# A two-layer graph kernel: ScalarE and TensorE programs written out instead of looped, with constant wait values

## What is computed

```python
def _L1_gnn_ref(x, spatial_encoding, edge_encoding, Wq, Wk, Wv, Wo):
    q = (x @ Wq.T).reshape(d, n, h)          # d = 128 heads, n = 3327, h = 8
    k = (x @ Wk.T).reshape(d, n, h)
    v = (x @ Wv.T).reshape(d, n, h)
    a = jnp.einsum('dnh,dmh->dnm', q, k) * scale
    a = a + spatial_encoding + edge_encoding
    a = jax.nn.softmax(a, axis=2)
    out = jnp.einsum('dnm,dmh->dnh', a, v)
    return out.reshape(n, h * d) @ Wo.T

h = jnp.maximum(_layernorm(x), 0.0);  x = x + _L0_gnn_ref(h, adj, L0_gnn_weight)
h = jnp.maximum(_layernorm(x), 0.0);  x = x + _L1_gnn_ref(h, adj, adj, Wq, Wk, Wv, Wo)
```

## Time and profile before

| | us |
|---|---|
| median of three executions | 14501.24 |
| lowest and highest | 14498.21, 14502.49 |
| the profiled execution, its own time | 14506.74 |
| its span, first to last instruction | 14504.7 |

### The profile page before, as it was taken

How to read it: one execution, slowest core, us unless ns; L and a number is a source line. 1 busy time by engine, 2 the same in 40 slices (tenths; PEclk the granted TensorE clock), 3 DMA queues, 4 the chain that set the end, 5 groups by cost and what they waited for, 6 DMA issues and landing times. The chain is left out here.

```text
span 14504.7 us, 430687 instructions
## 1 busy us (share of the span) xinstructions
PE 13822.4 (95%) x143755; PEld 4902.7 (34%) x143755; DVE 13807.1 (95%) x27589; ACT 13447.5 (93%) x30466; POOL 326.7 (2%) x945
## 2 busy tenths in 40 slices
PE   3889999999999999999999999999999999999999
PEld 2533333333333333333333333333333333333334
DVE  5589999999999999999999999999999999999993
ACT  1269999999999999999999999999999999999997
POOL 1100000000000000000000000000000000000000
PEclk7989999999999999999999999999999999999999
DMA  8965655656565565656556565655656565565653
GB/s 277 258 161 136 143 134 136 142 133 141 135 144 133 138 141 134 141 135 143 135 137 141 134 139 135 143 134 137 141 134 140 135 143 134 136 142 135 143 133 94
DMA packets 2075309, 2084.40 MB, mean 144 GB/s; under 512 B 818906, under 2 KB 1827809, under 8 KB 2066753
## 3 DMA queue, kind: packets, MB, share of 16 engines
q1 hardware_dynamic: 2069118, 2043.41, 58.8%
q10 hardware_dynamic: 4032, 13.31, 0.2%
HBM read 1922.23 MB, written 133.76 MB: 142 GB/s over the span
## 5 line engine op out<-in xcount | busy, mean ns | idle before, releaser
L235 DVE CUSTOM_DVE_ANT_0 X<-X,adj_row 128x832 f32<-128x832 f32 x13312 | 13314.5, 1048 | 111.8 <-PE X L257 74.7
L1000 ACT ACTIVATE prob<-S 128x416 f32<-128x416 f32 x26624 | 11895.8, 518 | 304.0 <-PE S L1068 121.7
L1068 PE MATMUL S<-q_blk,k_res 52*128 52x416 f16 x26624 | 6858.3, 344 | 41.5 <-ACT S L989 9.9
L1089 PE MATMUL O<-prob,v_pad 128*32 128x208 f32 (+1 forms) x87376 | 6727.3, 389 | 2.6
L257 PE MATMUL X<-mk,mq 40*128 40x416 f16 x26624 | 6270.4, 344 | 306.7 <-DVE m_part L235 279.8
L1068 PEld LDWEIGHTS S<-q_blk,k_res 52*128 52x128 f16 x26624 | 2214.9, 93 | 4250.3 <-ACT S L989 1454.4
L1089 PEld LDWEIGHTS O<-prob,v_pad 128*32 128x32 f32 x87376 | 1830.5, 108 | 2537.5 <-issue 2053.0
L257 PEld LDWEIGHTS X<-mk,mq 40*128 40x128 f16 x26624 | 1585.8, 93 | 2370.6 <-DVE m_part L235 1919.1
L235 DVE DVE_READ_ACCUMULATOR2_ANT m_part<- 128x1 f32 x13312 | 1884.5, 142 | 0.0
L989 ACT ACTIVATE S<-adj_key 128x416 f32<-128x416 f32 x3328 | 1757.2, 528 | 35.7
L207 POOL TENSOR_SCALAR m_neg<-m_full 128x16 f32<-128x16 f32 x208 | 52.5, 252 | 13065.5 <-DVE m_full L218 13065.4
(11 more groups left out here) (86 smaller groups left out, 1045.7 us busy)
## 6 DMA issues: line engine op xcount, KB each, us to landing
adj_key<-adj_by_key SPq DMA_DIRECT2D x3328, 208.0 KB, 3.4
adj_row<-in_adj SPq DMA_DIRECT2D x1200, 416.0 KB, 3.9
mk<-k_planes SPq DMA_DIRECT2D x1664, 104.0 KB
adj_row<-adj_tail SPq DMA_DIRECT2D x400, 416.0 KB, 3.9
mk<-k_planes SPq DMA_DIRECT2D x1664, 52.0 KB
row<-in_adj SPq DMA_DIRECT2D x47, 1663.5 KB, 8.0
adj_by_key<-aT SPq DMA_DIRECT2D x26, 1664.0 KB, 11.8
q_planes<-q_parts SPq DMA_DIRECT2D x26, 1024.0 KB, 15.0
```

The lines of the kernel that those rows point to most:

```text
L235: nc.vector.tensor_tensor_reduce(out=x_, in0=x_, in1=adj_row[gi % 4][:].rearrange("p (a b) -> p a b", a=2), scale=1.0, scalar=LOW, op0=ALU ...
L1000: nc.scalar.activation(prob[c % QR][:, d % 4, :], S[b][:, 0:WB], ACT.Exp, scale=2.0).then_inc(s_e[b], 1)
L1068: nc.tensor.matmul(S[b][:, 0:WB], k_res[base:base + KR, d // 2, s * P:(s + 1) * P], q_blk[n % 2][base:base + KR, d // 2, :], start=False, ...
L1089: done = nc.tensor.matmul(O[32 * d:32 * d + 32, cols], v_pad[:, s, 4 * q + d, :], prob[born(j, q) % QR][:, d, cols], start=first, stop=Tru ...
```

## The change

ScalarE and TensorE no longer call `spans` but `all_spans`, in which `k` is always a Python integer. Their programs become five times the loop's body and the tail; all their wait values become constants. SyncE keeps its loop, VectorE and GpSimd are as they were. The order of the matmuls, activations and DMAs, the semaphores and the values waited for stay the same.

```diff
+                def all_spans(first, last, body):
+
+                    for k in range(NG // 3):
+                        body(k, first, first + SPAN, 4 * SPAN)
+                    body(NG // 3, first, last, END)
+
...
-                        spans(act, FIRST, FIRST + END, body)
+                        all_spans(FIRST, FIRST + END, body)
...
-                        spans(pe, FIRST, FIRST + END + 8, body)
+                        all_spans(FIRST, FIRST + END + 8, body)
```

## The result

| | before | changed |
|---|---|---|
| median | 14499.5 us (15 runs) | 14533.9 us (15 runs) |
| lowest to highest | 14493.4 to 14513.7 | 14528.9 to 14541.8 |
| the profiled execution | 14506.7 | 14530.5 |
| its span | 14504.7 | 14528.1 |

The changed kernel takes 1.0024 times the time of the one before, with a 95% interval of 1.0016 to 1.0031: it is slower by 34 us. The forecast was 14526 us, in a range of 14505 to 14560; I had given 29% to slower by over 0.2%, and 60% to within it.

What follows compares the result with a forecast made beforehand. No single engine bounds it: TensorE, VectorE and ScalarE hand work round a ring. Added waits 58.0 us less returns 33.2 us gives +24.8 us on 14501.2: 14526 us, range 14505 to 14560.

Steps and rivals of the forecast that it cites:

- Part 1: TensorE's four loop returns: their stalls go, taking four segments from 460.0 to 426.8 us together, a gain of 33.2 us.
- boundary segments: The four stretches of 104 units between ScalarE output copies that hold a loop return; forecast from 460.0 to 426.8 us together.
- Part 2: TensorE's 32 ns and ScalarE's 35 ns register operations go; up to 3% if on the ring, but measured rate spoke against gain.
- Part 3: Constant waits give ScalarE two more separate semaphore waits a cycle before exponentials: 0.50 us a segment, adding 58 us.
- the added waits: Two buffer waits a cycle on ScalarE, formerly on register instructions, become separate; upper bound 0.12 us a cycle, 1.04 a segment.
- the third of the orders: Value orders repeat after three groups; the tail shows only one, whose 0.50 us a segment was taken for all.
- the ring: Hand-overs among VectorE sweep, TensorE matmuls and ScalarE exponential, freeing and filling banks; a delay there can lengthen the cycle without idle time.
- The sum: Whole kernel: 58.0 us added less 33.2 us removed, +24.8 us, between +13 and +33, giving 14526 us.
- The first: Rival: added waits cost nothing in the loop's groups, only the returns count; 14468 us, -0.23%; chance 12%.
- The second: Rival: both added waits bind in the other orders, at 1.04 us a segment; 14567 us, +0.46%; chance 5%.
- The third: Rival: at the returns another engine, such as SyncE, stops instead of TensorE at the same price; 14559 us; chance 5%.

## Why the prediction was right

**Part 1, the returns: right in size, with the wrong owner.** I had 33.2 us, from four boundary segments that would fall to 106.7 each. They did fall to 106.7, and 460.0 - 4 x 106.7 = 33.2. But I put it on TensorE alone, since its branch shows 4.25 us and ScalarE's 45 ns. TensorE alone written out gained nothing. The working took the segments' whole lengths and so was right for both engines together; that it fits is luck as far as the owner goes. The sentence that ScalarE "shows nothing of it" was wrong: it stopped as well, hidden behind TensorE. So did SyncE, for 3.7 to 4.6 us behind its branch of 50 ns at each return of the changed kernel, and there it cost nothing, as I had it: the boundary segments are at 106.7.

**Part 2, the register work: right.** No gain shows from its 32 and 35 ns: with TensorE alone written out the segments stay at 105.37 us for 105.34, and with ScalarE alone they grow.

**Part 3, the added waits: right in size to a tenth, the mechanism right in part.** I took 0.50 us for each of 115 segments, from the tail of the third of the orders that shows there. Over a whole pass it was 0.56 (105.90 for 105.34), and over all 115 segments 0.55, 63 us for my 57.5; in the second group of a pass, which the tail doesn't show, five segments took 529.9 us (4378.3 to 4908.2) for 527.3 before (4369.5 to 4896.8):

```profile
L1035 ACT ACTIVATE o_sb<-O x6: 517/525/552, 4378.3 to 4908.2; 128x416 f32<-128x416 f32 x6
```

It is also not ScalarE's alone, as I had it: 0.23 with ScalarE alone written out, 0.03 with TensorE alone and 0.56 with both; about half comes only when both are written out, and why is open. The explanation of two waits on the ring, alike, was too plain as well: both exponentials are late by 0.06 us, but moved singly the waits gave 35 and 8 us. And I took the separate wait to be an added one, where it is the scores' own. The tail gave nearly the right sum all the same, because it holds both engines' constants.

**The sum.** The two profiles differ by 14528.1 - 14504.7 = 23.4 us, which looks like my 24.8 and is partly luck. Up to the first copy of the tail they differ by 13700.1 - 13670.6 = 29.5 us, near 63 - 33 = 30. Behind it the profile before lost some 6 us again, and TensorE's granted clock fell there after the last sweeps (0.74 in 40 us, and 1.00 in the answering stretch of the changed kernel; the clock is the number behind the busy times):

```profile
14220.00:14260.00 40.00, 36.44 (x257) 8.76 (x256) 0.00 (x0) 31.90 (x74) 0.00 (x0) 0.74 0.19 50
```

```profile
14250.00:14290.00 40.00, 35.33 (x309) 10.40 (x301) 0.00 (x0) 38.27 (x90) 0.00 (x0) 1.00 0.23 59
```

Such a fall stands there in some runs' profiles and not in others, so it is no effect of the change that I could book. The medians differ by 34 us, so the forecast was 8 to 10 us short: some 6 of it are the mis-sized term of part 3 (63 for 57.5), and the rest no row accounts for; the executions of the kernel before lie between 14493 and 14514.

**The rivals.** The first (the added waits are free in the loop's groups) is refuted by the segments and by the extra waits at tight places. The second (both bind fully in the other orders) too: 105.98 us a segment in the second group, by 529.9 / 5, and not 106.4. The third (another engine stops instead) didn't come about when both were written out, but it is just what happened to TensorE alone: I had looked for it on SyncE, and it was ScalarE.

## What to carry to other kernels

An unrolled tail behind a loop is a run of the unrolled program: compare its rate with the loop's at the same place of the pattern before writing the loop out, and count a piece of finished work, not idle time. When engines hand work round a ring, look which instruction carries the wait that ends last. Where an instruction is needed just in time and has two waits, one of them can be moved ahead onto an instruction with slack; here that was worth 118 us, over three times what the unrolling cost. Moved too far ahead it is waited for itself. A stop seen on one engine may hide the same stop on its neighbour, so a gain from removing it should be booked only if all of them lose it.

## What the runs showed of the hardware

- Where an exponential on ScalarE has two waits, the one for the scores shows as a separate semaphore instruction of 17 ns, and the exponential answers the scores 0.06 us later (0.96 to 0.97 us from the start of the score matmul to the end of the exponential, for 0.90 to 0.91). With the other wait on a register instruction ahead of it, which takes 35 ns, the exponential waits for the scores itself and isn't late.
- ScalarE's jump back over some 2500 units stopped it for 4.7 us on average and 5.1 at most, as TensorE's did for 4.3 and 5.3, and its branch was recorded with 45 ns against TensorE's 4251: how long a branch is in the record doesn't tell what it costs here; the time to the next instruction in the queue does.
- Three waits a cycle that are always met cost 89 us in 14.4 ms at tight places, and nothing where the exponential had 0.24 us of slack or more.
